# Stacking the second low-rank products of the token mix into one single-pass product of 96 rows, with the stack made by DMA

## The reference

```python
xx = shifted(x) - x
lora = tanh((x + xx * maa_x) @ maa_w1).reshape(B, T, 5, 32)
m = einsum('btfd,fdc->fbtc', lora, maa_w2)      # five products with 32 terms each
xw, xk, xv, xr, xg = (x + xx * (maa_i + m_i) for i in (w, k, v, r, g))
r, k, v = xr @ Wr, xk @ Wk, xv @ Wv
g = tanh(xg @ gate_w1) @ gate_w2
w = time_decay + tanh(xw @ decay_w1) @ decay_w2
```

## Time and profile before

| what | value |
|---|---|
| median of 3 runs | 3557.01 us (3548.65 to 3559.22) |
| the profiled execution | 3554.4 us, span 3552.5 us |
| TensorE, VectorE busy | 2987.5 us (84%), 2561.8 us (72%) |
| ScalarE, GpSimd busy | 1266.6 us (36%), 1225.6 us (34%) |
| DMA | 115.05 MB, 16 engines busy 16% |
| mean granted TensorE clock | 0.94 of full |

### The profile page before, as it was taken

The page is one execution under the profiler, slowest core; times in us unless marked ns, Lnnn a source line. Parts: engine busy times, 40 slices in busy tenths (PEclk is TensorE's granted clock), DMA queues, the critical chain, the costliest instruction groups (busy, mean ns, idle before and its releaser), DMA issues.

```text
span 3552.5 us, 47119 instructions
## 1 busy us (share of the span) xinstructions
PE 2987.5 (84%) x17056; PEld 1838.9 (52%) x17056; DVE 2561.8 (72%) x5257; ACT 1266.6 (36%) x2625; POOL 1225.6 (35%) x1188
## 2 busy tenths in 40 slices
PE   2588889888888888898888888888978888798887
PEld 1235565355643566344763447535465354653656
DVE  4676687677875777857778568785697766976665
ACT  1263223722236222453125531265313642136322
POOL 0023451234512444124431345214452234422444
PEclk9699999999989999899998999899998999999999
DMA  4600032000510006000150002400023000330000
GB/s 132 104 2 13 18 63 53 2 16 15 81 35 14 10 10 100 16 14 10 28 96 2 13 15 40 79 2 13 18 45 70 2 13 18 49 67 2 1 1 13
DMA packets 68888, 115.05 MB, mean 32 GB/s; under 512 B 10795, under 2 KB 64075, under 8 KB 65531
## 3 DMA queue, kind: packets, MB, share of 16 engines
q1 hardware_dynamic: 68627, 111.51, 16.0%
HBM read 74.69 MB, written 33.65 MB: 30 GB/s over the span
## 4 chain that ended last, share of the span: by engine, by line
PE 48%; DVE 33%; issue 5%; POOL 5%; ACT 4%; DMA 2%; SPq 0%; DVEq 0%; POOLq 0%; ACTq 0%
DVE mxp L908 9%; PE PB L1247 7%; PE PB L1307 6%; PE PB L1232 5%; PE PB L1322 5%; PE PB L1218 4%; DVE arena L1094 4%; PE PB L1392 3%; PE PB L1361 3%; DVE arena L1102 3%; PE PB L1280 3%; DVE attn L831 3%; ACT arena L692 2%; PE PB L1449 2%; PE PB L1431 2%
## 5 line engine op out<-in xcount | busy, mean ns | idle before, releaser
L908 DVE TENSOR_REDUCE mxp<-PB 128x1 f32<-128x512 f32 (+3 forms) x1536 | 751.4, 549 | 153.6 <-PE PB L1218 84.5
L692 ACT ACTIVATE arena<-PB 128x512 f32<-128x512 f32 (+3 forms) x1536 | 649.1, 509 | 449.7 <-PE PB L1232 445.2
L1218 PE MATMUL PB<-arena 96*128 96x512 bf16 (+3 forms) x1536 | 509.3, 360 | 104.9 <-DVE mxp L908 64.1
L561 POOL TENSOR_SCALAR_AFFINE_SELECT arena<-arena 128x512 f32<-128x512 f32 x256 | 162.7, 636 | 997.1 <-ACT arena L692 996.8
L1232 PE MATMUL PB<-arena 99*128 99x512 bf16 (+3 forms) x1536 | 464.7, 342 | 26.8 <-DMA arena<-augT 19.6
L1218 PEld LDWEIGHTS PB<-arena 96*128 96x128 bf16 x1536 | 154.2, 101 | 424.0 <-DVE mxp L908 325.7
L1307 PE MATMUL PB<-xh,wgu 128*128 128x512 f32 x768 | 316.8, 412 | 47.0 <-DVE xl L975 30.7
L1247 PE MATMUL PB<-arena 128*32 128x512 f32 (+3 forms) x3072 | 338.6, 513 | 15.5 <-ACT attn L681 13.7
L571 POOL TENSOR_TENSOR hl<-arena,hh 128x512 fp32r<-128x512 f32 x192 | 248.1, 1294 | 241.8 <-ACT hh L717 237.6
L1307 PE MATMUL PB<-xl,wgu 128*128 128x512 f32 x768 | 311.3, 405 | 0.9 <-issue 0.9
L1465 PE MATMUL PB<-arena 128*128 128x128 f32 x1792 | 229.9, 283 | 91.4 <-DVE arena L1102 91.4
(11 more groups left out here) (137 smaller groups left out, 5275.7 us busy)
## 6 DMA issues: line engine op xcount, KB each, us to landing
arena<-parts SPq DMA_DIRECT2D x112, 256.0 KB, 9.7
parts<-arena SPq DMA_DIRECT2D x192, 128.0 KB
arena<-parts SPq DMA_DIRECT2D x16, 768.0 KB, 18.2
arena<-in_x SPq DMA_DIRECT2D x16, 512.0 KB, 4.9
arena<-parts SPq DMA_DIRECT2D x16, 512.0 KB, 20.7
xres<-in_x SPq DMA_DIRECT2D x16, 512.0 KB, 4.8
out<-xres SPq DMA_DIRECT2D x16, 512.0 KB, 3.4
wgu<-arena SPq DMA_DIRECT2D x2, 768.0 KB, 4.5
```

Of the source, the lines that this page charges most:

```text
L692: act.activation(pt[:, U % 3, h, 0:n], bank(b, "score", t)[:, 0:n], ACT.Exp, scale=DH ** -0.5).then_inc(act_emptied, 1)
L908: dve.reduce_max(mxp[:, g % 2, h, col:col + 1], bank(b, "max", g * NPC + k)[:, 0:n], axis=AX.X).then_inc(dve_emptied, 1)
L1218: last = mm(ps[:, 0:n], qst[0:AUG, h, 128 * i:128 * i + 128], kst[0:AUG, h, s0:s0 + n], start=True, stop=not diag)
```

## The change

It does five things.

1. `mw2` becomes 96 rows in float32r: rows 0 to 31 and 32 to 63 are the rounded weights, rows 64 to 95 the rest (weight minus rounded weight). The load is three DMAs of all five features instead of five; GpSimd's clearing of `mw2` goes, and two VectorE instructions make the parts before the first loop.
2. After tanh, ScalarE copies `lora` to `lora_hi` (rounded), VectorE subtracts into `lora_lo`: for l = 0 all 128 rows, for l = 1 the 32 rows of the fifth feature.
3. SyncE copies, for each token half and each mix, 32 rows of `lora_hi`, 32 of `lora_lo` and again 32 of `lora_hi` into the 96 rows of `mix_in[fi]`: 30 DMAs of 64 KB a batch.
4. A mix product is one float32r product with 96 contracted rows, which waits on `mix_ready`.
5. The order: mixes 0 to 7 go 0, 1, 4, 5, 2, 3, 6, 7 (`MIX_AT`), all behind the four first products; on VectorE the second rotation moves behind `differences`.

```diff
+MIX_AT = [0, 1, 4, 5, 2, 3, 6, 7] + list(range(8, 4 * NMIX))
...
         add(b, "ln2", (2, 3), "act")
-        add(b, "mix", (0, 1), "dve")
         add(b, "lora", (2, 3), "act")
-        add(b, "mix", range(2, 8), "dve")
+        add(b, "mix", MIX_AT[:8], "dve")
...
-        mw2 = sb("mw2", [128, NMIX, D])
+        mw2 = sb("mw2", [96, NMIX, D], f32r)
...
-                for f in range(NMIX):
-                    r = 32 * f if f < 4 else 96
-                    load(mw2[r:r + 32, f, :], b_mat[5][f, :, :])
+                for r in (0, 32, 64):
+                    load(w2[r:r + 32, :, :], b_mat[5].rearrange("f r n -> r f n"))
...
-                pool.memset(mw2[:, :, :], 0.0).then_inc(s_zero, 1)
...
+                dve.tensor_copy(mw2[:, :, :], w2).then_inc(s_cast, 1)
+                dve.wait_ge(s_cast, 1)
+                dve.tensor_tensor(mw2[64:96, :, :], w2[64:96, :, :], mw2[64:96, :, :].bitcast(f32), ALU.subtract)
...
+                    for f in (0, 1):
+                        cols = slice(HALF * f, HALF * f + HALF)
+                        sp.wait_ge(lora_low, 4 * b + 2 * f + 2)
+                        for mi, fi in enumerate(MIX_ORDER):
+                            l, r = (0, 32 * fi) if fi < 4 else (1, 96)
+                            for k, part in enumerate((lora_hi, lora_lo, lora_hi)):
+                                sp.dma_start(mix_in[fi][32 * k:32 * k + 32, 0, cols].bitcast(f32),
+                                             part[r:r + 32, l, cols].bitcast(f32)).then_inc(mix_ready[f][mi], 16)
+                    if b + 1 < NB:
                         parts_store(b + 1, range(4))
...
+                        for n in ns:
+                            l, f = n % 2, n // 2
+                            p = slice(96 * l, 128)
+                            wait_emptied(act, b, "lora", n)
+                            act.activation(lora_hi[p, l, HALF * f:HALF * f + HALF], lora[p, l, HALF * f:HALF * f + HALF],
+                                           ACT.Copy).then_inc(lora_high, 1)
...
+                    for f in (0, 1):
+                        act.wait_ge(mix_ready[f][NMIX - 1], 48 * (b + 1))
                     for n in range(4):
                         c, f = n % 2, n // 2
                         w = wdec[:, c, HALF * f:HALF * f + HALF]
...
+                    def lora_low_part(n):
+                        l, f = n % 2, n // 2
+                        p, cols = slice(96 * l, 128), slice(HALF * f, HALF * f + HALF)
+                        dve.wait_ge(lora_high, 4 * b + n + 1)
+                        dve.tensor_tensor(lora_lo[p, l, cols], lora[p, l, cols], lora_hi[p, l, cols].bitcast(f32),
+                                          ALU.subtract).then_inc(lora_low, 1)
+
+                    lora_low_part(0)
+                    lora_low_part(1)
                     if ahead:
-                        pair(rotary, b + 1, 0)
+                        rotary(b + 1, 0)
                     differences(2)
                     differences(3)
-                    for n in range(4 * NMIX):
-                        mixed(n)
+                    if ahead:
+                        rotary(b + 1, 1)
+                    lora_low_part(2)
+                    lora_low_part(3)
+                    for n, k in enumerate(MIX_AT):
+                        mixed(k)
...
-                        wait_emptied(pe, b, "lora", 2 * f + 1)
+                        pe.wait_ge(mix_ready[f][mi], 48 * (b + 1))
                         wait_bank(pe, b, "mix", n)
                         mm(bank(b, "mix", n)[:, :], mw2[:, fi, 128 * co:128 * co + 128],
-                           lora[:, fi // 4, HALF * f:HALF * f + HALF], start=True, stop=True).then_inc(filled, 1)
+                           mix_in[fi][:, 0, HALF * f:HALF * f + HALF], start=True, stop=True).then_inc(filled, 1)
...
-                            pe.wait_ge(mix_added, 20 * b + 4 * n0 + 2 * f + 2)
+                            pe.wait_ge(mix_added, 20 * b + MIX_AT.index(4 * n0 + 2 * f + 1) + 1)
```

More of the change, by code:

```diff
@@ L262, in build @@
         th = region(6144, 1024)
+        lora_hi = rounded("lora_hi", 7168, [128, NC, T])
+        lora_lo = rounded("lora_lo", HIGH + 11264, [128, NC, T])
+        mix_in = [rounded(f"mix_in{fi}", at, [96, 1, T]) for fi, at in enumerate((11264, 12288, 13312, 14336, 4096))]
         wdec = ct(region(7168, 2048))
@@ L326, in build @@
         xxx_done = sem("xxx_done")
+        lora_high = sem("lora_high")
+        lora_low = sem("lora_low")
+        mix_ready = [[sem(f"mix_ready{f}_{mi}") for mi in range(NMIX)] for f in (0, 1)]
         mix_added = sem("mix_added")
@@ L381, in _ @@
                     load(wqkv[:, :, D * k:D * k + D], w.rearrange("(c p) n -> p c n", p=128))
-                sp.wait_ge(s_zero, 7)
+                sp.wait_ge(s_zero, 6)
                 for h in range(NH):
@@ L417, in _ @@
                 sp.wait_ge(s_ones, 16)
-            NLOAD = 3 + NH + 2 + 4 + 1 + NMIX + 4 + 1 + 2 + 4 + 3
+            NLOAD = 3 + NH + 2 + 4 + 1 + 3 + 4 + 1 + 2 + 4 + 3
             @block.gpsimd
@@ L584, in _ @@
                     pool.wait_ge(qd_zeroed, 2 * b + 2)
-                    for n in range(4 * NMIX):
+                    for j, n in enumerate(MIX_AT):
                         c, f = n % 2, n // 2 % 2
@@ L589, in _ @@
                         pool.tensor_tensor(a, a, xT[:, c, 1 + HALF * f:1 + HALF * f + HALF], ALU.add).then_inc(mix_added, 1)
-                        if ahead and n == 3:
+                        if ahead and j == 3:
                             ln_scale(0, b + 1, 1)
@@ L1404, in _ @@
                     transpose_x(2, (2, 3))
-                    mix_items(0, 2)
                     lora_item(2)
                     lora_item(3)
-                    mix_items(2, 6)
+                    for n in MIX_AT[:8]:
+                        mix_item(n)
                     hidden("dech", 64, DLOW, 0, 0)
```

6 lines of the change are left out of this document (3 added, 3 removed).

## The result

The changed kernel takes **3567.95 us** (median of 15 runs, 3561.0 to 3576.47) against 3555.32 of the kernel before (15 runs, 3548.65 to 3560.97) on the same chip. The ratio is 1.0033, 95% interval 1.0025 to 1.0042: slower by 12.6 us, and the interval lies on both sides of the 0.3% that I took as the bound. The profiled execution took 3568.7 us with a span of 3567.0, 14.5 more than before. The mean granted clock fell from 0.94 to 0.918.

The account below looks back on a forecast made before the run. TensorE (84% busy), with VectorE dense beside it, was taken to bound each batch up to the end of the v products. Seven batches +3.9, last batch -2, start +2.2 made +4.1: 3558.5, said as 3560; range 3537 to 3582.

Parts of the forecast that it names:

- rival B: Faster: the granted clock does not fall, not even before the low-rank products; 2.65 us a batch, 3537 us; chance 0.21.
- rival C: Slower: TensorE stays at the lower clock from 805.4 into the gate branch; 2.75 us a batch, 3576 us; chance 0.17.
- signs of being wrong: Wrong if VectorE does not idle, DMA landings exceed 9 us, or clock around second `hidden` item is 1.00 in all batches.
- The single pass: TensorE's twenty mix products a batch: 0.23 us apart instead of 0.86; 12.6 us work saved a batch, 101 in all.
- Rival E: Slower: the 96-row mix product runs in two passes, 0.43; 1.6 us a batch on the path, 3571 us; chance 0.06.
- VectorE's delay: VectorE waits behind its second rotation for rounding copies, done at 792.95; the normalisation ends at 808.6, 5.1 us later.
- The transfers: SyncE's fifteen DMAs per token half: each issue near 0.59, landing 1.9 us later, hidden by 5.6 us of cover.
- Rival D: Slower by DMA: landing of 12.0 us makes mix 2's stack 4.3 too late; decides from 9; 3587 or 3575; chance 0.09.
- The clock: TensorE's two new pauses, 5.3 and 4.2 us: one half-rate loss of 2.2 at 805.4, +1.0 us a batch on path.
- the base: Per batch at the end of the v products, clock aside: 7.5 saved, less 5.1 delay and 1.9 wait, gain 0.45.
- The last batch: No next-batch rotations in the way, so TensorE decides: -3.9 us, taken as -2 with one clock loss of 2.2.
- Before the first loop: VectorE's new subtraction (1.4) and cast (0.7 to 1.4) of 1280 columns: +2.2 us; loads and clearing counted as zero.

Follow-up runs that it names:

- experiment 2: Changed kernel without the 30 stack DMAs a batch, products reading `lora_hi` in place (part of the computation left out): 3576.14 us, ratio 1.0054 to the kernel before.
- experiment 7: experiment 3 with 6 or 15 extra 64 KB stores ahead of the second half's stack transfers in SyncE's queue: 3588.68 us, one run.
- experiment 5: experiment 3 with VectorE's remainders ahead of the second low parts, statistics right behind them, and 16 instead of 8 unread products between `hidden` items: 3533.76 us.
- experiment 3: Changed kernel with unread filler products in TensorE's three pauses (20, 16 and 8) to hold the clock up: 3545.48 us, ratio 0.9969 to the kernel before.
- experiment 4: Kernel before the change with 18 unread filler products in its one pause of 5.53 us: 3529.48 us, ratio 0.9928 to the kernel before.
- experiment 6: experiment 5 with the mix products in plain float32 over the same 96 rows instead of float32r: 3589.65 us, ratio 1.0092 to the kernel before.
- experiment 8: Changed kernel with only the 20 filler products of the first pause, before the second low-rank products: 3546.69 us, one run.
- experiment 9: Changed kernel with VectorE's remainders and statistics ahead of the second half's low parts, plus 20 filler products in the first pause: 3524.16 us, ratio 0.9912.
- experiment 10: experiment 5 with 4 filler products between the `hidden` items in place of 16: 3529.7 us, ratio 0.9921 to the kernel before.

## Why the prediction was right, and where not

The time lies 8 us above the forecast of 3560 and inside the range. The range is 45 us wide and held rivals B and C as well, so the time alone confirms little. The side was missed by a little: no change beyond 0.3% had the best chance, and 0.33% came. By the prediction's own bound of 1.5 us a batch the 1.83 measured is on the side of rival C, slower by the clock, though not by C's route: the new pauses cost 1.20, near the forecast's 1.0. None of its signs of being wrong came; the normalisation ended 24.7 after the second half's low-rank products began (23 to 25), the mark 61.6 to 64.6 after them, beyond the 60 to 63 in two batches. Point by point, in the prediction's order.

**The single pass** was as said: the mixes in the row at 812.38 follow at 0.26 on average (1.17 less the last one's 0.40, over three), the last three of them 0.23 apart, as expected. Rival E, with 0.43, is out.

**VectorE's delay** was the prediction's centre and held. The second low part was to end at 792.95 by the second batch of before and ended at 793.95 (795.06, less the 1.11 by which this batch starts later); the wait in front of it was to be 4.5 and was 5.13. Kept warm, so with no clock in it, the normalisation comes 37.87 - 32.48 = 5.4 later (5.1 predicted), the gate branch 2.9 (2.6), the r products 2.5 (2.0), and the mark 0.0 (-0.45). Each step carries on an error of 0.3 to 0.5. Some 0.25 of it is there when the second half's low-rank products start, 1.04 sooner than before (15.97 after the stage's start in place of 17.01) and not 1.3; and ScalarE's rounding copies take 0.63 each, where I had 0.57.

**The transfers.** Issues stand 0.63 apart (0.6), the landing is 1.9 at the least, 2.0 in the median and 2.5 at most:

```profile
L526 SPq DMA_DIRECT2D mix_in<-lora_hi x160: 507/590/768, 349.1 to 3399.2; - x160
...
DMA to landing us min/median/max: 1.9/2.0/2.5
```

Rival D needed 9. Experiments 2 and 7 show the cover: none of the transfers' time reaches the normalisation, and it would take 5.5 us more to do so, where the prediction had 5.6. The Trainium skill, DMA: Bandwidth & Descriptors, section "Issuing engines are not separate DMA queues", calls the time to start a DMA usually small relative to the DMA itself. With 0.59 beside 2.0 this case disagrees: fifteen issues take 9.4 us, and the last transfer of a half is issued 8.8 after the first.

**The clock was the term that was mis-sized.** I had taken one loss of 2.2 for the pause that was there before, in both kernels, and +1.0 for the new pauses. The first is right for the kernel before (2.24), the second for the new pauses (1.20). What failed is the step between: that filling the old pause gives the changed kernel back the same. It gave 2.85. At the gate branch it is 2.36, hardly more than the 2.24 before, and that is a mean of 2.7 in five batches, where the lower level held for 10.2 us, and 1.5 in two, the first and third, where it held for 6.8. The pause was 6.21 in all seven, after 5.53 before. I had written that it would grow, against rival B, and had not put a price on it; but its length alone doesn't set the price, and what does no run shows. The other 0.5 is the half-rate stretch at 826 to 831, 1.7 us in each of two batches, for which the prediction had no term; it goes when the first pause is filled, and comes in five batches of experiment 2. What brings it stays open. So a stage loses 0.0 (the base) + 0.6 (0.1 and 0.5, the two parts of the old pause's extra price) + 1.2 (the new pauses) = +1.8 instead of -0.45 + 1.0 = +0.55, and seven stages lose 12.8 us instead of 3.9. The Trainium skill, TensorE: Matmul & The Clock Gate, section "Why this matters for your kernels", advises against pauses between matmul bursts. Both new pauses were followed by half rate: the first, of 4.95, agrees with the page; the second, of 2.75, is shorter than those it speaks of. Rival C, which was that rule, had the kind of the loss right and its size too high (2.75 a batch).

**The last batch**: -2 predicted, -1.4 measured, with no next batch in the way. No run holds the clock of that batch alone, so what its 0.6 is made of is open. **Before the first loop**: +2.2 predicted, 0 measured in these two traces. VectorE's two new instructions cost 0.82 and 1.48, as sized:

```profile
30.70 0.82 DVE L441 CAST mw<-arena 96x1280 fp32r<-96x1280 f32 x1 [30.70 <-DMA arena<-in_f_w_down]
31.56 1.48 DVE L443 TENSOR_TENSOR mw<-arena,mw 32x1280 fp32r<-32x1280 f32 x1
33.06 2.56 DVE L444 CAST arena<-arena 128x4608 f32<-128x4608 int32 x1
```

but the cast behind them starts where it started before, since the loads landed 2.34 us sooner. Before:

```profile
33.04 2.56 DVE L436 CAST arena<-arena 128x4608 f32<-128x4608 int32 x1 [33.04 <-DMA arena<-in_f_w_down]
```

I had counted the transfers and the clearing as zero, between -1 and +1. SyncE's fourth issue comes at 3.50 in both kernels that clear `mw2` and at 2.39 in all ten that don't, and two issues fewer give 0.9 more; that makes 2.0 of the 2.34. Some luck is in the 0: over all twelve traces that cast starts at 32.7 and 33.0 with the clearing and at 32.9 to 34.7 without it, 0.7 later on average. **Outside the stages** I had put nothing. The stretches from a mark to the next stage grew by 5.3 in sum, and what lies behind the last mark shrank by 2.3. The instructions there are unedited; their clock stretches differ from batch to batch, and no run here says why.

Against 4.1 us predicted for the span this makes 4.1 + 8.9 (stages) + 0.6 (last) - 2.1 (ahead of the first stage) + 3.0 (outside) = 14.5. That the median came out 8 us off and not 10 or more is in part luck: the loads gave back two thirds of what came up outside the stages, and the prediction had priced neither.

## What to carry to other kernels

When an edit puts a wait on an in-order queue, look at what was doing the queue's work in that time. Here 3 us of VectorE's work stood behind a wait of 5.1 that it could have filled, and moving it ahead was worth 1.1%, where the change as it was built was worth nothing. Work taken off an engine that then pauses is not only not gained: what is left ran slower here, so price the pauses that a saving opens, and the growth of the ones that are there. A few products that nobody reads bought 0.7% in the unchanged kernel, but only as long as they end before what the engine waits for does; beyond that they sit on the path like any other work, 1.7 us a batch for the 16 of experiment 5.

## What was not expected of the hardware

- The lower clock level came also where TensorE had no long pause: ahead of the stretch at 826 to 831 (0.68) its waits were 0.70 and 0.96 us. That stretch came in the second and fifth batch alone, whose marks (80.60, 80.50) are 1.5 to 3.0 above the others. The same two waits (0.69 and 0.96) stand in the other five batches, where no such stretch follows.
- In experiments 3, 4, 6 and 8 the marks of the seven batches agree within 0.1 us; in the changed kernel they spread over 3.05, in the kernel before over 0.7. Filling the first pause isn't enough for that: in experiments 5, 9 and 10 it is filled too, and they spread over 1.7 to 1.9. Each time the batches that differ have the lower clock level at another place or for longer. A spread between equal stages is a sign of the clock.
- VectorE's two remainders take 1.21 and 1.58 us where GpSimd's additions run beside them, and 0.69 each where none does, in each of the first three batches of all twelve kernels.
- The filler bought more than the stage shows. In the kernel before, 7 x 2.24 = 15.7 us were to be had, and the median fell by 27.7; from mark to next stage each stretch was 1.2 to 3.3 shorter as well, some 12 us in all.
